# A graph layer on one core: two chunks per tile from rows of x staged ahead instead of one, and TensorE's idle products out

## What is computed

```python
def _forward(feats, ...):
    deg_out = jnp.clip(segment_sum(ones, src, num_segments=n), 1.0)
    deg_in = jnp.clip(segment_sum(ones, dst, num_segments=n), 1.0)
    h = feats * rsqrt(deg_out)[:, None]
    m = segment_sum(h[src], dst, num_segments=n) * rsqrt(deg_in)[:, None]
    x = m @ W_gc + b_gc + (feats @ W_res + b_res)
    core = _moe_ff(x, Wg, bg, w1, b1, w2, b2)      # 64 experts, top 2
    y = x + core
    mean = jnp.mean(y, axis=0)
    var = jnp.mean((y - mean) ** 2, axis=0)
    return (y - mean) * rsqrt(var + BN_EPS) * gamma + beta
out = layernorm(x + _forward(x, ...))
```

## Time and profile before

| | us |
|---|---|
| median of 3 executions | 3360.32 |
| lowest, highest | 3358.57, 3361.39 |
| span of the profiled execution | 3782.8 |
| stage 1 in the profiled execution | 0 to 394.5 |
| stage 2, first to last gather from h_table | 394.5 to 2630.2 |
| TensorE busy, POOL busy (of the span) | 2867.3, 2109.8 |

### The profile page before, as it was taken

The page is one execution under the profiler, slowest core; times in us unless marked ns, Lnnn a source line. Parts: engine busy times, 40 slices in busy tenths (PEclk is TensorE's granted clock), DMA queues, the critical chain, the costliest instruction groups (busy, mean ns, idle before and its releaser), DMA issues. The chain is left out here.

```text
span 3782.8 us, 61265 instructions
## 1 busy us (share of the span) xinstructions
PE 2867.3 (76%) x15295; PEld 2136.6 (56%) x15296; DVE 2006.0 (53%) x7025; ACT 1197.5 (32%) x2890; POOL 2109.8 (56%) x2156
## 2 busy tenths in 40 slices
PE   3245778787777877777777777778699999999950
PEld 3234445555545545555554555555588989888840
DVE  5369444444544444454444444444555555555598
ACT  3368112222222222222212222212244444444428
POOL 5722666666666666666666666665355555555500
PEclk7557888998998888989889888989899999999985
DMA  7622534444444434444344444434444454444387
GB/s 245 188 68 89 175 114 137 117 141 119 142 144 119 136 117 137 148 117 138 118 138 121 146 137 119 137 109 126 142 139 138 149 161 136 148 136 151 99 312 233
DMA packets 309520, 537.64 MB, mean 142 GB/s; under 512 B 47197, under 2 KB 220381, under 8 KB 307698
## 3 DMA queue, kind: packets, MB, share of 16 engines
q0 software_dynamic: 102160, 273.85, 24.8%
q1 hardware_dynamic: 206766, 259.99, 20.8%
q10 hardware_dynamic: 436, 1.85, 0.1%
HBM read 418.03 MB, written 121.75 MB: 143 GB/s over the span
## 5 line engine op out<-in xcount | busy, mean ns | idle before, releaser
L1427 POOL DMA_INDIRECT work<-h_table,src_cols x1529 | 1456.6, 953 | 785.1 <-issue 419.1
L1820 PE MATMUL ps<-work 128*128 128x257 f32 x3322 | 1056.8, 400 | 36.9 <-issue 35.0
L1820 PEld LDWEIGHTS ps<-work 128*128 128x128 f32 x3322 | 621.1, 198 | 290.7 <-issue 114.4
L1691 PE MATMUL ps<-none_w,none 128*128 128x512 bf16 x1369 | 534.2, 390 | 14.1 <-issue 13.6
L2091 PEld LDWEIGHTS ps<-xst,work 128*128 128x128 f32 x3648 | 443.4, 192 | 28.9 <-issue 17.9
L2091 PE MATMUL ps<-xst,work 128*128 128x128 f32 x3648 | 447.4, 276 | 11.6 <-issue 11.6
L1966 POOL DMA_INDIRECT picked<-ys,places x228 | 249.2, 1093 | 357.5 <-DVE ys L2036 334.8
L2098 PE MATMUL ps<-work,hid 128*128 128x256 f32 x1824 | 436.6, 382 | 0.3
L1722 PE MATMUL ps<-w_conv,turned 128*128 128x320 f32 x392 | 173.7, 579 | 268.5 <-ACT turned L1380 181.1
L1947 ACT ACTIVATE hid<-ps,b_cols 128x128 f32<-128x128 f32 x912 | 304.1, 367 | 186.2 <-PE ps L2091 119.2
L2098 PEld LDWEIGHTS ps<-work,hid 128*128 128x128 f32 x1824 | 329.0, 190 | 46.3 <-ACT hid L1947 10.5
(11 more groups left out here) (309 smaller groups left out, 4244.3 us busy)
## 6 DMA issues: line engine op xcount, KB each, us to landing
work<-in_L_gnn_w_dram SPq DMA_DIRECT2D x128, 512.0 KB
picked<-work SPq DMA_DIRECT2D x14, 1792.0 KB
work<-h_table,src_cols POOLq DMA_INDIRECT x1529
pk<-picked SPq DMA_DIRECT2D x13, 1792.0 KB
x_ahead<-work SPq DMA_DIRECT2D x105, 128.0 KB
work<-x_ahead SPq DMA_DIRECT2D x105, 128.0 KB
acc<-m_base SPq DMA_DIRECT2D x14, 903.0 KB
x_beta<-xr_x SPq DMA_DIRECT2D x98, 128.0 KB
```

Source lines behind the costliest of these rows:

```text
L1427: pool.indirect_dma_start(out=got[:, c % RING, 0:D], out_offset=None, in_=h_table[:, :], in_offset=bass.IndirectOffsetOnAxis(ap=src_cols[: ...
L1691: nc.tensor.matmul(ps[:, 7, :], none[:, :], none_w[:, :], start=False, stop=False)
L1820: mm = nc.tensor.matmul(ps_flat[:, bank(t, k, w[0])], hot[:, (2 * t + (k >= HALF)) % HOTS, k % HALF if k >= HALF else k, :], got[:, c % RI ...
```

## The change

`AHEAD_AT`, the extra chunks, `f_table` and all that handled them are taken out. In their place each of the 91 tiles has two ahead chunks, at places 8 and 14. So stage 1 stages 182 chunks in place of 105, and stage 2 gathers 1,452 in place of 1,529. The factors of the pair are picked at two places of TensorE's order, behind chunks 4 and 10; the codes of both are spread by one product of 256 columns. `IDLE` becomes 0.

```diff
-AHEAD_AT = 8
-EXTRA = 14
-EXTRA_FIRST, EXTRA_EVERY, EXTRA_AT = 10, 6, 12
+PAIR_AT = (8, 14)
+PAIR = len(PAIR_AT)
...
-        staged_chunks = [PER * (FIRST_AHEAD + n) + AHEAD_AT for n in range(AHEAD)] + extra_chunks
+        staged_chunks = [PER * (FIRST_AHEAD + n) + at for n in range(AHEAD) for at in PAIR_AT]
...
-                    keep_ahead(0, AHEAD + EXTRA)
+                    keep_ahead(0, AHEAD * PAIR)
...
-                    pool.wait_ge(f_kept, 16)
-                    for n, c in enumerate(extra_chunks):
-                        pool.indirect_dma_start(out=f_edge[:, READY + n:READY + n + 1], out_offset=None, in_=f_table[:, :],
...
-        PICK_AT = 10
+        PICKS_AT = (4, 10)
...
-        IDLE = 1
+        IDLE = 0
...
                     if among(slot + 1):
-                        load_ahead(slot + 1 - FIRST_AHEAD)
+                        load_ahead(PAIR * (slot + 1 - FIRST_AHEAD))
                     if slot >= 2 and within(slot):
                         load(slot)
+                    if among(slot + 1):
+                        load_ahead(PAIR * (slot + 1 - FIRST_AHEAD) + 1)
...
                     if among(slot + 1):
-                        scale_ahead(slot + 1 - FIRST_AHEAD)
-                    if extra_of(slot + 1) is not None:
-                        scale_extra(extra_of(slot + 1))
+                        for k in range(PAIR):
+                            scale_ahead(PAIR * (slot + 1 - FIRST_AHEAD) + k)
...
-                    if c in ahead or c in extra_chunks:
+                    if c in ahead:
                         continue
...
-                    nc.vector.tensor_scalar(diag[:, :], ident[:, :], ahead_f[:, 1, n:n + 1], None, ALU.mult).then_inc(diag_set, 1)
+                    nc.vector.tensor_tensor(diag[:, :, :], ident[:, :].unsqueeze(1).broadcast_to([P, PAIR, P]),
+                                            ahead_hi[:, i, :].unsqueeze(2).broadcast_to([P, PAIR, P]), ALU.mult).then_inc(diag_set, 1)
...
+                    if among(slot + 2):
+                        edge_factors(slot + 2 - FIRST_AHEAD, 0)
                     if within(slot - 1):
                         evict(slot - 1)
                         degree(slot - 1)
                     if among(slot + 3):
                         code_hots(slot + 3 - FIRST_AHEAD)
                     if among(slot + 2):
-                        edge_factors(slot + 2 - FIRST_AHEAD)
+                        edge_factors(slot + 2 - FIRST_AHEAD, 1)
...
-                        if k == PICK_AT and among(t + 2):
-                            pick_factors(t + 2 - FIRST_AHEAD)
-                        if k == PICK_AT and among(t + 3):
+                        if k in PICKS_AT and among(t + 2):
+                            pick_factors(t + 2 - FIRST_AHEAD, PICKS_AT.index(k))
+                        if k == PICKS_AT[-1] and among(t + 3):
                             spread_codes(t + 3 - FIRST_AHEAD)
```

More of the change, by code:

```diff
@@ L319, in gnn_layer @@
                 aggregate(nc, x, W_res, b_gc, b_res, W_gc, Wg, bg, b1, beta, h_table, x1_rows, x_beta, picked, m_base, flag_i, base_out, zeros_out, y_total, acc3, work, ident, ones,
-                          iota_f, place_lo, src_cols, rel_cols, where, valid, f_edge, f_lanes, x_ahead, extra_f_in, early_set, table, base_of, b1_cols, load_weights, ps,
+                          iota_f, place_lo, src_cols, rel_cols, where, valid, f_edge, f_lanes, x_ahead, early_set, table, base_of, b1_cols, load_weights, ps,
                           N=N, D=D, X=X, H=H, KD=KD, KH=KH, AW=AW, CH=CH, PER=PER, EARLY=EARLY, LATE=LATE, NT=NT, LAST=LAST)
@@ L514, in columns_and_degrees @@
 def columns_and_degrees(nc, x, h_table, rows_s, rows_d, rows_1, src_early, starts, chunk1, lane0, acc3, ident, ones, iota_f, src_cols, rel_cols, tile_off,
-                        where, base_out, f_out, f_table, work, f_edge, f_lanes, x_ahead, early_x_in, extra_f_in, early_set, ps, N, D, CH, CL, RJ, NT, LAST, STEPS, AW, PIECES, GROUPS, HI0, PER, EARLY,
+                        where, base_out, f_out, work, f_edge, f_lanes, x_ahead, early_x_in, early_set, ps, N, D, CH, CL, RJ, NT, LAST, STEPS, AW, PIECES, GROUPS, HI0, PER, EARLY,
                         LATE, general):
@@ L660, in _ @@
                     for q in range(STAGED):
[L661 removed]
+                        sp.wait_ge(staged_out[q], 16 * ((AHEAD * PAIR - q + STAGED - 1) // STAGED))
             @block.gpsimd
@@ L1100, in aggregate @@
 def aggregate(nc, x, W_res, b_gc, b_res, W_gc, Wg, bg, b1, beta, h_table, x1_rows, x_beta, picked, m_base, flag_i, base_out, zeros_out, y_total, acc3, work, ident, ones, iota_f,
-              place_lo, src_cols, rel_cols, where, valid, f_edge, f_lanes, x_ahead, extra_f_in, early_set, table, base_of, b1_cols, load_weights, ps,
+              place_lo, src_cols, rel_cols, where, valid, f_edge, f_lanes, x_ahead, early_set, table, base_of, b1_cols, load_weights, ps,
               N, D, X, H, KD, KH, AW, CH, PER, EARLY, LATE, NT, LAST):
@@ L1140, in aggregate @@
         ps_flat = ps[:, :, :].rearrange("p b n -> p (b n)")
[L1141 to L1144, removed]
+        FACTORS = 4 * PAIR
+        ahead = [PER * (FIRST_AHEAD + n) + at for n in range(AHEAD) for at in PAIR_AT]
+        assert READY <= ahead[0] and ahead[-1] < CH
+        fetched = [c for c in range(READY, CH) if c not in ahead]
         fetch_of = {c: i for i, c in enumerate(fetched)}
[L1146 to L1150, removed]
+        ahead_src = src_cols[:, PER * FIRST_AHEAD:PER * (FIRST_AHEAD + AHEAD)].rearrange("p (t k) -> p t k", k=PER)
+        ahead_lo = t2("ahead_lo", [P, AHEAD, PAIR], F32)
+        ahead_hi = t2("ahead_hi", [P, AHEAD, PAIR], BF16)
+        f_ahead = t2("f_ahead", [P, FACTORS], F32)
+        diag = t2("code_diag", [P, PAIR, P], BF16)
+        code_hot = t2("code_hot", [P, PAIR, P], F32)
         hot_x = t2("hot_x", [P, 2, P], F32)
```

105 lines of the change are left out of this document (45 added, 60 removed).

## The result

| | before | after |
|---|---|---|
| median of 12 runs, us | 3,359.14 | 3,369.38 |
| lowest, highest | 3,357.29, 3,361.76 | 3,365.52, 3,371.70 |
| ratio, 95% interval | | 1.0029 (1.0021 to 1.0037) |

The account below looks back on a forecast made before the run. POOL's gathers, 1.254 us apart, were taken to bound stage 2. The terms -96.6 (stage 2), +96.6 (staging), +3 (VectorE) and +3 (staging beside VectorE) gave 3,360.3 + 6 = 3,366 us, range 3,320 to 3,420.

Parts of the forecast that it names:

- Reading the gap between profile and median: Histogram and stage 2: the 422.5 us between profile and median are standstills that timed executions mostly lack.
- rival A: Stage 1: a histogram nearly as long as profiled hides the added staging; 96.6 us gained, 3,264 us; chance 0.13.
- the reconstruction: Whole timed execution before the change: stage 1 300, stage 2 1,917, rest 1,153, sum 3,370 us, 0.3% above the median.
- Staging +96.6 and +3: Stage 1: 77 more uncovered staging gathers cost 96.6 us, and 3 more for those that meet a working VectorE.
- Stage 2 -96.6: Stage 2: 77 fewer gathers at 1.254 us save 96.6 us, since POOL sets the pace.
- VectorE's wider steps +3: Stage 2 factors: the added VectorE work is hidden on VectorE but slows POOL's gathers by 3 us.
- the rule on the shared port: VectorE and GpSimd: an exclusive port lock blocks descriptor writes; wider diagonal could cost a piece of 31 us, by row 3.
- The factor gathers gone, 0: Stage 1: removing 14 factor gathers, 18 us of POOL, gains 0, as the writes to h_table end later.
- The rest unchanged: Behind stage 2: the rest of the kernel, 1,153 us, had no term for a change.
- the partial cover: Stage 1: some 30 of the 97 us of added staging are hidden, 3,333 us; chance 0.12.
- Rival B: Stage 2: without idle products TensorE's clock falls and TensorE overtakes POOL; +92 us, 3,458; chance 0.15.
- Rival C: Stage 2: TensorE waits at chunk 14 for rows or factors; POOL's lead leaves 0 us, no chance of its own.

Follow-up runs that it names:

- experiment 1: The kernel before, no edit, profiled a second time: 3,361.9 us, span 3,359.9.
- experiment 2: The kernel before with 77 more chunks staged in stage 1 that nobody reads, stage 2 as before: 3,456.7 us, 1.0295.
- experiment 4: The changed kernel with pairs in 60 tiles, 120 chunks staged and 1,514 gathers: 3,353.4 us, 0.9994 to the kernel before.
- experiment 5: The changed kernel with pairs in 30 tiles, 60 chunks staged and 1,574 gathers: 3,385.7 us, 1.0087 to the kernel before.
- first mixed kernel: The changed kernel with writes to h_table cut into 98 tiles, put between the last 98 writes to x_ahead on SP's queue: 3,345.3 us, 0.9962.
- second mixed kernel: The changed kernel with the 98 h_table writes spread over the last 82 writes to x_ahead, beginning behind 100 staged chunks: 3,337.8 us, 0.9941.

## Why the prediction was right

The time, the direction and the main mechanism came out: 3,366 forecast, 3,369.4 measured, two terms of about 100 us that cancel. The last 10 us, by which the kernel is slower, came by another way than the sum had it. By its steps:

- **Reading the gap between profile and median** as standstills that timed executions lack: right. In the second trace the histogram ends at 220 (217 forecast), the last staging gather comes at 247 (252), the first gather from `h_table` at 292 (300). That 252 fell so near 247 is in part luck: the staging started at 76.3 and not at 68.5, and the 15 us that I gave to a gather blocked by the scaling of x weren't there (no staging gather of this trace takes over 1.7 us). And what follows stage 2, taken from the profile with standstills as 1,153 us, was 1,142, which is most of the 10 us by which the reconstruction lay too high. Reading the gap was the step on which all hung; the histogram's end at 342.9 in the earlier trace rows, taken as it stands, would have given rival A and a gain of 97 us.
- **Staging +96.6 and +3:** 99.0 (experiments 1 and 2). The pace is (346.9 - 247.0) / 77 = 1.30 us, as some of the gathers run beside VectorE until 262.
- **Stage 2 -96.6:** -103.5. POOL does set the pace, but the idle products weren't free there. I gave their removal 0; in the kernel before it is 9 us of stage 2, in the changed one 2. Of the 9, POOL's shorter waits for TensorE (14.4 to 6.7 us) are 8; its gathers also take 7 us less (1,456.7 to 1,450.0) and its issues 5 more (454.9 to 460.3), and why is not shown. The mean over 98 tiles hid the few places where TensorE held POOL, which I had seen in the earlier trace rows and taken for rare.
- **VectorE's wider steps +3:** no such cost shows. A gather takes 1,378.84 / 1,452 = 0.950 us, against 1,456.74 / 1,529 = 0.953 before and 1,449.97 / 1,529 = 0.948 before without idle products. None of the changed kernel's in stage 2 takes over 1.19 us, so the wider diagonal with two inputs from SBUF, against which the prediction turned the rule on the shared port, held no gather up. One was held by VectorE only in stage 1 (last section).
- **The factor gathers gone, 0:** right. In the second trace they run from 248.5 to 269.5, beside the writes to `h_table`, and none takes 15 us.
- **The rest unchanged:** wrong. 1,141.7 us behind the last gather became 1,152.8, all of it in stage 3. The forecast had no term for it, and without it the two others would have made 99.0 - 103.5 = -4.5, a kernel of 3,355, as the one with idle products is (3,355.6). So that the kernel came out slower at all hangs on stage 3, and the nearness of 3,366 to 3,369 is in part chance: in stage 2 I was off by 10 us one way (-93.6 with VectorE's term, -103.5 measured), in stage 3 by 11 the other.
- **Rival A and the partial cover:** out (experiments 2, 4). **Rival B:** the clock falls, but to 0.94, and no time goes with it in stage 2; the slower side came by another way. TensorE is busy 1,501 of 1,823 us there, 82%, not the 66% that I had worked out. **Rival C:** its wait is there and costs nothing, as the prediction had it: TensorE's picks of factors wait 66 times for VectorE's sum, 15.3 us in all and at most 0.8 at once, and never for the scaled rows of an ahead chunk; POOL waits 10.4 us for TensorE in 29 places, less than before. The picks' line among the waits of the changed kernel (total, times, longest):

```profile
PE ps L1761 <- DVE junk L1542: 15.3, 66, 0.8
```

**What stays open:** why stage 3 takes 914 to 919 us in six of the kernels and 901 to 905 in the others. All six have pairs in 91 tiles (and so an `x_ahead` of 182 chunks) and no idle products, both at once, and none of the others has both. Each of the two alone is cleared: idle products are missing in the kernel before with `IDLE = 0` and in that with pairs in 60 tiles (902.9 in both), and pairs in 91 tiles with idle products take 900.6. An `x_ahead` of 182 chunks is cleared only in a kernel that has idle products (903.5, experiment 2); with that size and neither idle products nor pairs none was run. It isn't SP's order (914 to 915 in both mixed kernels without idle products), and no shift by 8 or 32 products cures it. That it is the length of TensorE's program is argued and not shown. A larger shift, and where the tables lie in HBM, weren't tried.

## What to carry to other kernels

Work that is moved into a stage is free only until the next thing on the same queues is ready; count what stands behind it, and where both places are paced by the same engine, expect a zero. When a profile is longer than the timed runs by hundreds of us, find the standstills that make up the difference first, and ask what cover the kernel has without them. The gain here came with letting a queue's later, independent writes go between the staged ones: 1.0029 became 0.9941, and 0.9914 with the idle products back. Whether the kernel before, with its 105 staged chunks, would gain as much from the same mixing wasn't run, so what the pairs add to the mixing is not known.

## What the runs showed of the hardware that I had not expected

- The same run of 65 VectorE instructions (the scaling of x) stops POOL's gathers or doesn't. In the changed kernel the gathers beside it start every 1.25 us, and VectorE needs 20.39 us for its run; in experiment 5, where POOL has nothing to do then, VectorE needs 17.16. In the first trace of before one gather took 15.47 us while VectorE needed 17.16, and in the first mixed kernel one took 13.81 while VectorE needed 17.57. Both long ones began after a pause of POOL, while VectorE was already at it, and both ended 0.8 us behind VectorE's run (368.10 behind 367.28, 245.21 behind 244.39); VectorE's run of the mixed kernel is the first line below, the other two are gathers of the changed kernel. In the changed kernel, the second trace of before and the second mixed kernel POOL was in an unbroken row of gathers when the scaling began, and none was held:

```profile
226.82 17.57 DVE L777 TENSOR_SCALAR acc<-acc,f_out 128x256 f32<-128x256 f32 x65 [0.19 <-DVE f_out L979]
```

```profile
226.88 0.95 POOL L686 DMA_INDIRECT work<-in_x_dram,src_cols  x1 [0.30 <-issue]
228.13 0.95 POOL L686 DMA_INDIRECT work<-in_x_dram,src_cols  x1 [0.30 <-issue]
```

  The Trainium skill, "SBUF — State Buffer", section "SBUF: two separate sides", says that the port pair that VectorE (in a mode that uses both of its ports) shares with GpSimd is held by whichever of the two starts first, for the whole instruction, while the other waits. By that rule, the traces agree in part: a gather that came after a pause of POOL, with VectorE at it, had to wait. But the page's lock is for one instruction. Here a gather was held over dozens of them, and in the unbroken row the next gather began 0.30 us after the one before, each time, with VectorE at work in between. What decides there no run shows.
- A stage that no edit touches can change by 12 us of 905. A term for it belongs in the range of a forecast that works with differences of 10.
